# Fused two-layer attention and expert kernel: the order of one DMA queue, the order of GpSimd's adds, and the sums of the last block

## The reference

```python
scores = jnp.einsum('bhsd,bhtd->bhst', q, k) * scale
attn = jax.nn.softmax(scores, axis=-1)
o = jnp.einsum('bhst,bhtd->bhsd', attn, v_c)
...
x = x + _L0_attn_ref(_layernorm(x, axis=-1), ...)
x = x + _L0_ffn_ref(_layernorm(x, axis=-1), ...)
```

## Time and profile before

| | before |
|---|---|
| median of 3 runs | 770.61 us (770.42 to 771.03) |
| profiled execution | 775.4 us, span 773.7 us |
| granted TensorE clock, mean | 0.993 |
| busy share: PE, DVE, ACT, POOL | 95%, 81%, 61%, 75% |
| attention loop, first scores to last | 38.0 to 510.3 us |

### The profile page before, as it was taken

The page is one execution under the profiler, slowest core; times in us unless marked ns, Lnnn a source line. Parts: engine busy times, 40 slices in busy tenths (PEclk is TensorE's granted clock), DMA queues, the critical chain, the costliest instruction groups (busy, mean ns, idle before and its releaser), DMA issues.

```text
span 773.7 us, 12688 instructions
## 1 busy us (share of the span) xinstructions
PE 737.8 (95%) x4214; PEld 468.8 (61%) x4214; DVE 626.3 (81%) x1305; ACT 473.2 (61%) x1067; POOL 577.4 (75%) x478
## 2 busy tenths in 40 slices
PE   7999999999999999999999999999799999999997
PEld 6655555545545555555554555456556689778885
DVE  7889899998999898999999999933887736876564
ACT  4377666767767666776776766663677841454443
POOL 6489889988989989898998898911689861445554
PEclk9999999999999999999999999997999999999999
DMA  7200000000000000000000000003000000000000
GB/s 155 73 2 1 2 2 2 2 3 1 1 3 1 1 2 2 1 2 2 2 2 3 1 1 2 1 22 93 1 1 0 2 1 2 0 1 16 0 14 27
DMA packets 36616, 8.71 MB, mean 11 GB/s; under 512 B 26580, under 2 KB 35813, under 8 KB 36552
## 3 DMA queue, kind: packets, MB, share of 16 engines
q1 hardware_dynamic: 35272, 7.80, 5.0%
q10 hardware_dynamic: 1280, 0.12, 0.1%
HBM read 6.53 MB, written 1.05 MB: 10 GB/s over the span
## 4 chain that ended last, share of the span: by engine, by line
PE 51%; POOL 12%; issue 10%; DMA 9%; SPq 9%; DVE 5%; ACT 3%; POOLq 0%; DVEq 0%
PE ps L1385 11%; PE ps L1371 10%; SPq L451 9%; DMA q_cols<-nmx 8%; PE ps L1429 8%; POOL hid_lo L917 7%; PE ps L1440 4%; PE ps L1775 4%; PE ps L1413 4%; ACT den_sb L563 2%; POOL nrm L899 2%; POOL hid L899 1%; PE ps L1358 1%; PE ps L1359 1%; DVE mx L971 1%
## 5 line engine op out<-in xcount | busy, mean ns | idle before, releaser
L858 POOL TENSOR_TENSOR part<-part,prob 128x512 f32<-128x512 f32 x248 | 329.3, 1328 | 44.7 <-DVE part L986 17.2
L971 DVE TENSOR_REDUCE mx<-ps 128x1 f32<-128x512 f32 x492 | 310.4, 681 | 36.3 <-PE ps L1371 32.5
L577 ACT ACTIVATE prob<-ps 128x512 f32<-128x512 f32 x512 | 271.1, 604 | 95.6 <-PE ps L1385 95.6
L1385 PE MATMUL ps<-q_cols,key 128*128 128x512 f32 x512 | 217.1, 427 | 13.1 <-DMA q_cols<-nmx 10.8
L1371 PE MATMUL ps<-key,q_rows 128*128 128x512 f32 x512 | 201.3, 397 | 0.8 <-DVE key L957 0.4
L1385 PEld LDWEIGHTS ps<-q_cols,key 128*128 128x128 f32 x512 | 95.5, 188 | 123.0 <-issue 49.9
L1429 PE MATMUL ps<-prob,val 128*32 128x512 f32 x1024 | 123.3, 598 | 0.0
L1371 PEld LDWEIGHTS ps<-key,q_rows 128*128 128x128 f32 x512 | 95.9, 188 | 19.2 <-DVE mx L965 1.4
L917 POOL TENSOR_TENSOR hid_lo<-hid,hid_hi 128x512 fp32r<-128x512 f32 x44 | 56.8, 1295 | 49.6 <-ACT hid_hi L734 49.6
L853 POOL TENSOR_TENSOR part<-prob 128x512 f32<-128x512 f32 x62 | 79.7, 1285 | 4.8
L1429 PEld LDWEIGHTS ps<-prob,val 128*32 128x32 f32 x1024 | 26.7, 109 | 60.9 <-issue 59.6
(11 more groups left out here) (278 smaller groups left out, 1085.8 us busy)
## 6 DMA issues: line engine op xcount, KB each, us to landing
den<-den_sb SPq DMA_DIRECT2D x124, 2.0 KB, 2.1
X<-in_L_attn_h_t_dram SPq DMA_DIRECT2D x4, 256.0 KB, 4.4
out_dram<-X SPq DMA_DIRECT2D x4, 256.0 KB, 2.3
w_raw<-in_L_ffn_w_g_dram SPq DMA_DIRECT2D x1, 704.0 KB, 4.4
w_raw<-in_L_ffn_w_u_dram SPq DMA_DIRECT2D x1, 704.0 KB, 7.6
w_raw<-in_L_ffn_w_d_dram SPq DMA_DIRECT2D x1, 704.0 KB, 9.0
w_o<-in_L_attn_W_O_dram SPq DMA_DIRECT2D x1, 512.0 KB
w_out<-in_L_attn_W_out_dram SPq DMA_DIRECT2D x1, 512.0 KB, 5.0
```

The lines of the kernel that those rows point to most:

```text
L577: act.activation(prob[:, g % RING, :], ps[:, g % 3, :], ACT.Exp, scale=SCALE).then_inc(s_exp, 1)
L858: pool.tensor_tensor(total, total, p[x], ALU.add).then_inc(s_sum, 1)
L971: dve.tensor_reduce(mx[:, n % 2, c % TPB, at:at + 1], ps[:, BANK["rows", 2 * lin + j], :], AX.X, ALU.max).then_inc(s_mrd, 1)
L1385: pe.matmul(ps[:, g % 3, :], key[:, n // NB % KBUF, t * P:(t + 1) * P], q_cols[:, n % NB, :], start=True, stop=True).then_inc(s_sc, 1)
```

## The change

It has three parts. SyncE's queue gets the shift row of block n ahead of the denominators of block n - 2. GpSimd adds tiles 2 and 3, and tiles 6 and 7, into a new buffer `pair` and adds that to the total, so its ten adds of a block are five on tiles 0 to 7, and five behind VectorE's first part add; ScalarE's exp of tile 0 accordingly waits for five sums in place of six. In the last block GpSimd makes six adds on tiles 0 to 7 and TensorE sums the two results with two matmuls (`first_totals`), so that `last_totals` is left for groups 2 and 3; the norms of the first two quarters stand behind all sums of block 30, `totals` of block 30 stays in slot 3, the first norm's transposes move from slot 2 to slot 4, and the last denominators and output stand ahead of the two small transposes.

```diff
--- before.py
+++ after.py
@@ -197,6 +197,7 @@
         KB_AT = H * C1
         prob = sb("prob", [P, RING, BLK])
         part = sb("part", [P, 2, NG, BLK])
+        pair = sb("pair", [P, 2, BLK])
         den_sb = sb("den_sb", [P, BLK])
         den = sb("den", [P, 2, NG, TPB])
         mx = sb("mx", [P, 2, TPB, 4])
@@ -452,8 +453,6 @@
 
                 for n in range(NBLK):
                     k = n % NB
-                    if n >= 2:
-                        denominators(n - 2)
                     sp.wait_ge(s_sel, n + 1)
                     if n < NB:
                         sp.wait_ge(s_qcol, k + 1)
@@ -462,6 +461,8 @@
                     with nc.allow_non_contiguous_dma("128 x 4 words into one row"):
                         sp.dma_start(q_cols[SH:SH + 1, k, :].bitcast(F32).rearrange("a (p i) -> a p i", i=TPB),
                                      nmx[:, n % 2, :].bitcast(F32)).then_inc(s_shift, 16)
+                    if n >= 2:
+                        denominators(n - 2)
 
                 denominators(NBLK - 2)
 
@@ -570,7 +571,7 @@
                     act.wait_ge(s_sc, g + 1)
                     if g >= RING and t == 0:
                         act.wait_ge(s_pv, NW * (n - 1) + 1)
-                        act.wait_ge(s_sum, ADDS * (n - 1) + 6)
+                        act.wait_ge(s_sum, ADDS * (n - 1) + 5)
                     elif g >= RING and t == NT // 2:
                         act.wait_ge(s_pv, NW * n)
                         act.wait_ge(s_sum, ADDS * n)
@@ -614,7 +615,7 @@
                         if t == 12 and n == 0:
                             folded()
                         exponential(n, t)
-                        if n == NBLK - 1 and t == 8:
+                        if n == NBLK - 1 and t == 10:
                             ln0_act(act, 0, 3)
                 ln0_act(act, 1, 4)
                 sums_out(NBLK - 1)
@@ -839,33 +840,67 @@
                 add_bias(2)
                 add_bias(3)
 
-                def sums(n, g):
-
-                    total = part[:, n % 2, g, :]
-                    p = [prob[:, (NT * n + t) % RING, :] for t in range(NG * g, NG * (g + 1))]
-                    done = ADDS * n + 3 * g - sum(x < g for x in VSUM)
-                    if n >= 2 and g == 0:
+                def ready(n, tile):
+                    pool.wait_ge(s_exp, NT * n + tile + 1)
+
+                def summed(n, count):
+
+                    pool.wait_ge(s_sum, ADDS * n + count)
+
+                def add(out, a, b):
+                    pool.tensor_tensor(out, a, b, ALU.add).then_inc(s_sum, 1)
+
+                def first_sums(n):
+
+                    def tile(t):
+                        return prob[:, (NT * n + t) % RING, :]
+
+                    total = [part[:, n % 2, g, :] for g in range(2)]
+                    if n >= 2:
                         pool.wait_ge(s_ones, n - 1)
-                    if g in VSUM:
-                        pool.wait_ge(s_sumd, len(VSUM) * n + VSUM.index(g) + 1)
-                    else:
-                        pool.wait_ge(s_exp, NT * n + NG * g + 2)
-                        pool.tensor_tensor(total, p[0], p[1], ALU.add).then_inc(s_sum, 1)
-                        done += 1
-                        pool.wait_ge(s_sum, done)
-                    for x in (2, 3):
-                        pool.wait_ge(s_exp, NT * n + NG * g + x + 1)
-                        pool.tensor_tensor(total, total, p[x], ALU.add).then_inc(s_sum, 1)
-                        done += 1
-                        pool.wait_ge(s_sum, done)
+                    ready(n, 1)
+                    add(total[0], tile(0), tile(1))
+                    ready(n, 3)
+                    add(pair[:, 0, :], tile(2), tile(3))
+                    if n < 2:
+                        columns(n + 2)
+                    ready(n, 5)
+                    add(total[1], tile(4), tile(5))
+                    summed(n, 2)
+                    add(total[0], total[0], pair[:, 0, :])
+                    ready(n, 7)
+                    add(pair[:, 1, :], tile(6), tile(7))
+
+                def last_sums(n):
+
+                    def tile(t):
+                        return prob[:, (NT * n + t) % RING, :]
+
+                    total = [part[:, n % 2, g, :] for g in range(NG)]
+                    pool.wait_ge(s_sumd, len(VSUM) * n + 1)
+                    ready(n, 10)
+                    add(total[2], total[2], tile(10))
+                    summed(n, 5)
+                    add(total[1], total[1], pair[:, 1, :])
+                    ready(n, 11)
+                    summed(n, 6)
+                    add(total[2], total[2], tile(11))
+                    pool.wait_ge(s_sumd, len(VSUM) * n + 2)
+                    ready(n, 14)
+                    add(total[3], total[3], tile(14))
+                    ready(n, 15)
+                    summed(n, 9)
+                    add(total[3], total[3], tile(15))
 
                 for n in range(NBLK - 1):
-                    for g in range(NG):
-                        sums(n, g)
-                        if g == 0 and n < 2:
-                            columns(n + 2)
-                        if n == NBLK - 2 and g >= 2:
-                            ln0_pool(pool, g - 2)
+                    first_sums(n)
+                    last_sums(n)
+                    if n == NBLK - 2:
+                        ln0_pool(pool, 0)
+                        ln0_pool(pool, 1)
+                first_sums(NBLK - 1)
+                summed(NBLK - 1, 5)
+                add(part[:, 1, 1, :], part[:, 1, 1, :], pair[:, 1, :])
                 pool.memset(anchors2[:, :], 0.0).then_inc(s_aside, 1)
 
 
@@ -1443,14 +1478,21 @@
                 def last_totals(g):
 
                     n = NBLK - 1
-                    if g == 0:
+                    if g == 2:
                         bank_read(("sums", n))
                     pe.wait_ge(s_exp, NT * n + NG * (g + 1))
                     for x in range(NG):
                         last = pe.matmul(ps[C * x:C * (x + 1), BANK["sums", n], :], ones_v[:, :], prob[:, (NT * n + NG * g + x) % RING, :],
-                                         start=(g == 0), stop=(g == NG - 1))
+                                         start=(g == 2), stop=(g == NG - 1))
                     if g == NG - 1:
                         last.then_inc(s_ones, 1)
+
+                def first_totals():
+
+                    n = NBLK - 1
+                    pe.wait_ge(s_sum, ADDS * n + 6)
+                    for g in range(2):
+                        pe.matmul(ps[C * g:C * (g + 1), BANK["sums", n], :], ones_v[:, :], part[:, n % 2, g, :], start=False, stop=False)
 
                 def last_denominators():
 
@@ -1569,20 +1611,18 @@
                         if slot == 7 and n == NBLK - 2:
                             output(n - 1)
                         if n == NBLK - 1:
-                            if slot == 2:
-                                last_totals(0)
+                            if slot == 3:
+                                totals(n - 1)
+                            elif slot == 4:
                                 bank_read(("norm", 0))
                                 ln0_pe(pe, 0, 3)
-                            elif slot == 3:
-                                totals(n - 1)
-                            elif slot == 4:
-                                last_totals(1)
                             elif slot == 7:
                                 output(n - 1)
                                 last_totals(2)
                                 bank_read(("norm", 1))
                                 ln0_pe(pe, 1, 4)
                                 weigh(n, range(2 * NG, 3 * NG))
+                                first_totals()
                 last_totals(3)
                 weigh(NBLK - 1, range(3 * NG, NT))
 
@@ -1590,10 +1630,10 @@
                 pe.wait_ge(s_exp, NT * NBLK)
                 pe.wait_ge(ld_l1a, 16 * N_LD_L1A)
                 pe.wait_ge(ld_l0, 16 * N_LD_L0)
+                last_denominators()
+                output(NBLK - 1)
                 pe.transpose(ps[0:A, 0, 0:A], anchor[:, :], ident[0:A, 0:A])
                 pe.transpose(ps[:, 0, AT_GATE:AT_GATE + E], gate0[:, :], ident[0:E, 0:E]).then_inc(s_an_ps, 1)
-                last_denominators()
-                output(NBLK - 1)
                 for j in range(E // 2):
                     last = pe.transpose(ps[:, 7, j * P:(j + 1) * P], up0[:, 2 * j:2 * (j + 1), :].rearrange("p e c -> p (e c)"), ident[:, :])
                 last.then_inc(s_up_ps, 1)
```

## The result

The changed kernel takes 749.0 us (median of 4 runs, 747.98 to 749.3), the kernel before 770.82 beside it: a ratio of 0.9715, 95% interval 0.9698 to 0.9732. It is faster, by 21.8 us. The forecast of 758.0 had the direction; its range ended at 749.5, 0.5 us above what was measured. So the prediction was wrong: its price of a GpSimd add was too high, and most of the miss follows from that one term.

A forecast was written before the change was run, and what follows sets the result against it. TensorE, waiting for the shift row, bounded the loop; GpSimd would after the change. Loop gain 15.3 less 1.2 for the last block took 775.4 to 761.3, or 756.5 at the median; 758.0 was taken, range 749.5 to 767.5.

The forecast's parts named there:

- part 2: GpSimd's ten adds in pairs: 13.65 us a block plus 0.62 for the lock, 14.27, so GpSimd ends the loop at 412.
- part 3: Last block: TensorE sums fewer tiles directly, but GpSimd's lag delays norms and adds; 1.2 us later than before.
- 2.3 us of room: GpSimd may start a block at 5.3 us, drifting to 7.64, before ScalarE's exponential of tile 8 waits for it.
- D1: VectorE's first part add in a block: 0.68 us alone, 1.79 when begun right behind the start of a GpSimd add.
- pause: GpSimd's stop of 0.68 us per block, its seventh add waiting for VectorE's first part add; forecast to go.
- Rival B: GpSimd's pause at VectorE's first part add stays, 14.58 us a block, loop 420.5, kernel 765.0; chance 0.19.
- Rival A: TensorE stays the bound and GpSimd keeps up: 752.7 us, at best 749.4 if no row lands late; chance 0.25.
- late landings: Shift rows landing after up to 3.38 us instead of 1.94: 9.1 us of the loop, 3.3 expected to stay.
- Part 1: Shift row issued 0.96 us earlier in SyncE's queue: 11.6 us and 5.8 of 9.1 go, TensorE's loop 409.9.
- Part 2's lock: SBUF port shared by VectorE and GpSimd: VectorE waits out a GpSimd add, GpSimd loses only 0.31 us per meeting.
- D2: VectorE's second part add in a block; a GpSimd add meeting it takes 1.61 us in place of 1.29.
- Rival C: Both VectorE part adds take their whole 0.68 us from GpSimd: 15.01 a block, kernel 777.5 us; chance 0.08.

The follow-up runs named there:

- run 4: Changed kernel with every GpSimd add again waiting for the semaphore of the add before it: 767.87 us, ratio 0.9946 to the kernel before.
- run 1: Kernel before with only SyncE's queue order changed, shift row ahead of the four den DMAs: 766.14 us, ratio 0.9917.
- run 9: Changed kernel with three waits on the preceding GpSimd add put back (adds 2, 4 and 5): 756.52 us, ratio 0.9816 to the kernel before.
- run 2: Kernel before with only GpSimd's adds of blocks 0 to 30 in the new order, old queue and last block: 770.37 us, ratio 0.9988.
- run 3: Kernel before with only the last block changed, old queue and old adds: 769.14 us, ratio 0.9967.
- run 7: Kernel before with the shift row first and its six early GpSimd adds alternating between two totals, no pairs: 767.25 us, ratio 0.9947.
- run 8: Changed kernel with one wait put back, GpSimd's second add waiting for its first: 748.64 us, ratio 0.971 to the kernel before.

## Why the prediction was wrong, and where it was right

**The step that failed** is the price of GpSimd's adds in part 2: "The same 10 adds a block, at 1.37 us each (339.87 to 343.97 is three): 13.65 us, no more and no fewer." The 1.37 was read as the price of an add. It was the price of an add with a wait for the one right before it: the add is busy 1.29 in either kernel, the next starts 1.23 to 1.25 after it when it needn't wait. The change removes most of these waits, since an add into `pair` or another total stands between two adds of a chain. The diff shows it (each `pool.wait_ge(s_sum, done)` gone; of the four `summed` in their place only the one before the tenth add waits for the add right before it), and the rows showed a pitch longer than the busy time; I took the pitch and didn't ask what filled it. Putting the waits back (run 4) returned 18.9 of 21.8 us. In the loop that was 412 forecast against 406.35.

The forecast of 758.0 lies 9.0 above the result. Of this 5.7 is the loop, 2.3 the seam behind it (part 3, where the lag came from the same price), and 1.5 the clock stretch, of whose 4.8 us only 3.3 were taken off; the start of the kernel adds 0.6, and its rest takes 1.0 off.

**The room that was not there.** The second half of that step let GpSimd lag until ScalarE's exp of tile 8, 2.3 us of room. It never came to that. In run 4, the slowest, GpSimd's first add of a block stands at 6.1 us (6.4 at most) from block 4 to 27, while exp of tile 8 comes at about 8.1; it doesn't drift. Where GpSimd overlaps D1, the block grows, in runs 1, 4 and 9 within the first six blocks, through VectorE's late maxima and TensorE's key matmul (run 1). That path was not in the sum. The 14.27 us forecast for a block is what run 9 shows, but by luck: it rested on D1 falling into the fourth add and the pause going, and in run 9 D1 falls into the fifth and a pause of 0.63 stays. Rival B's 14.58 is close to run 1's 14.56 and run 4's 14.65, and its "pause kept" is what they show. B's loop, 420.5, is near the 422.5 of run 4: it would have been about right for a kernel with self-waits.

**Rival A is what happened,** at its best corner: TensorE the only bound, 406.6 forecast for the loop with no row too late, 406.35 measured. What stood against it, GpSimd's 14.27 above TensorE's 14.07, fell with the 1.37. It had the bound right but not the cause: it counted on late landings, and not on cheaper adds. The 749.4 for it was left outside the range by 0.1, though A had a chance of 0.25.

**Part 1 held.** The row goes out 0.20 us after its reduce begins (0.2 forecast), 0.4 us of each block went, and the four den DMAs behind it show no wait. Of the late landings 3.3 us were to stay; none did. The cause may be the queue order itself: of 32 rows, 7, 5 and 6 landed after over 2.5 us in the three kernels with four den DMAs right ahead (before, runs 2 and 3), at most 2 in each of the nine others, where the latest took 2.61 us. That is an association; what delays such a row was not tested. Alone, part 1 gave 0.8% and not the 20.7 us (2.7%) that TensorE stood to gain: the ring took the rest.

**Part 2's lock** held better than the prediction read it. VectorE's D1 waits out GpSimd's add: 1.42 to 1.55 in runs 1, 4 and 7. The other way, GpSimd's add at D2 takes 1.74 in place of 1.29 after the change, a loss of 0.45. D2 in VectorE's timeline of the block above:

```profile
362.65 0.78 DVE L1021 TENSOR_TENSOR part<-prob 128x512 f32<-128x512 f32 x1
```

Its first 0.24 us fall into the GpSimd add that ends at 362.89; the next add, from 362.85, overlaps D2 by 0.58 and loses 0.45. In run 1 the overlap is 0.47 and the loss 0.32. So GpSimd loses the time that it meets D2, less 0.13 to 0.15, and not D2's whole length. The exclusive lock of the Trainium skill ("SBUF — State Buffer", two separate sides) agrees with both directions to within these 0.15; the prediction's "only half agrees" compared the loss with D2's length and not with the overlap. Rival C, which took the whole 0.68 of both part adds from GpSimd, is out: no ring ran at 15.01, and in the blocks read D2 cost GpSimd 0.32 to 0.45.

**Part 3** was forecast 1.2 us later. The last block came 1.5 earlier, of which the moved transposes take 0.5 back: last block and stretch to the gate are 22.02 + 14.95 before, without the clock, and 20.49 + 15.43 after, 1.05 less. The +1.2 was GpSimd's lag, and there was none. Without it the prediction had 0.5 earlier, so the other terms were short by about 0.5. TensorE's and GpSimd's timelines in block 31, against the earlier trace rows:

```profile
480.13 1.07 PE L1475 MATMUL ps<-part,ones_v 128*32 128x512 f32 x8 [0.21 <-POOL part L851]
...
482.61 0.63 PE L338 MATMUL ps<-ident,hn 128*128 128x128 f32 x4 [0.75 <-DVE hn L332]
...
479.95 0.23 POOL L312 TENSOR_SCALAR vare<-mv 128x4 f32<-128x4 f32 x1
...
490.45 0.60 PE L1495 MATMUL ps<-part,ones_v 128*32 128x512 f32 x2
```

GpSimd ends block 30 at 479.98, 5.3 us into block 31 and not 7.5; `totals` waits 0.21, the norm 0.75 (1.44 before), and in front of the two matmuls on `part` TensorE is not idle.

**From profile to median.** The 4.8 us by which the profiled execution stood above the median were held by the prediction to be late landings, perhaps. They are the size of the half-speed stretch behind the loop, and run 3's profile has the same pair. Beside the runs, executions of the kernel before at 774.6 to 775.2 us have a mean granted clock of 0.992 or 0.993, those at 770.2 to 770.9 of 0.995 to 0.999. The page showed the stretch and the prediction allowed a microsecond or two for it. Carried over whole, the sum would have been 756.5.

## What to carry to other kernels

When instructions of one engine follow each other more slowly than they are long, ask what stands between them before using the pitch as a price: a wait for one's own predecessor is a cost that reordering independent work removes. Where two engines hold each other up, as VectorE's part add and GpSimd's adds do here, look for the time at which one must be done so that the other is not held; on one side of it a few tenths of a us were free here (run 8), on the other they closed a ring of three engines (runs 1, 4 and 9). Two edits that each move little alone can be worth far more together when each is hidden behind what the other removes (0.8% and 0.1% alone, 2.6% together); so test them in pairs.

## What the runs showed of the hardware

- A GpSimd add of 128x512 float32 is busy 1.29 us, and the next begins 1.23 to 1.25 after its start (changed kernel). A wait for the semaphore of the add just ahead makes that 1.37 where it is the first or only wait between the two (before, runs 4 and 9), and 1.44 where a wait for ScalarE's tile stands ahead of it (runs 8 and 9).
- VectorE's small norm steps under GpSimd's adds are slowed far more than its part adds: four of 128x128 take 1.12 us with only GpSimd's own 128x4 norm steps beside them and 5.02 beside four adds. TensorE had no need of them for another 1.3 us, so it cost nothing here. VectorE's timeline in block 31 of the changed kernel:

```profile
481.34 1.12 DVE L332 TENSOR_SCALAR hn<-X,mv,rstd 128x128 f32<-128x128 f32 x4 [1.91 <-POOL rstd L314]
482.68 5.02 DVE L332 TENSOR_SCALAR hn<-X,mv,rstd 128x128 f32<-128x128 f32 x4 [0.22 <-POOL rstd L314]
```
